# A graph kernel's edge counts with packed block words, a wait for the pair ahead, and degree sums by DMA

## The reference

```python
edge_index = jnp.stack([src, dst])
# layer 0: an MLP on each edge, batch norm over all edges, sum by target
edge_features = jnp.concatenate([x[src], x[dst]], axis=1)
h = edge_features @ W1.T + b1
h = jax.nn.relu(_batchnorm(h, g1, be1))      # mean and variance over the edges
h = h @ W2.T + b2
edge_updates = jax.nn.relu(_batchnorm(h, g2, be2))
x_out = jax.ops.segment_sum(edge_updates, dst, num_segments=x.shape[0])
# layers 1 to 3: GCN forward and backward, four resonant steps, 8-head attention over the same edges
x = _layernorm(x + layer(x, edge_index), axis=-1)
```

## Time and profile before

| | us |
| --- | --- |
| median of three runs | 4106.11 |
| profiled execution, its own time | 4105.13 |
| its span | 4103.4 |
| counts, from 80 to | 849 |
| aggregation, to | 977 |
| edge stage, to | 1469 |

### The profile page before, as it was taken

One profiled execution on the slowest core, in us unless ns is written; L12 is line 12 of the kernel. 1 busy time (PEld: TensorE's weight loads), 2 busy tenths in 40 slices (PEclk: granted clock), 3 DMA queues, 4 the chain that ended last, 5 costly groups with the idle time before them and its releaser, 6 DMA issues. The chain is left out here.

```text
span 4103.4 us, 83720 instructions
## 1 busy us (share of the span) xinstructions
PE 3401.6 (83%) x20358; PEld 1667.9 (41%) x20359; DVE 2769.9 (68%) x3759; ACT 1589.8 (39%) x2188; POOL 1042.3 (25%) x1132
## 2 busy tenths in 40 slices
PE   3777777677899978888989994898899989979995
PEld 1333333333444557777455553333322233332223
DVE  6887766622666666664121215899799989989995
ACT  2134555520222246553011111311288831218883
POOL 2887774565666412220000001000100000000000
PEclk8989999978999999998999996999899999989998
DMA  2245665667777668776747774211144331113343
GB/s 62 89 160 189 215 226 191 215 210 248 248 251 242 222 228 252 233 212 193 263 136 253 251 258 98 88 56 56 50 136 141 115 95 56 56 38 117 108 132 70
DMA packets 359412, 662.49 MB, mean 161 GB/s; under 512 B 134549, under 2 KB 221715, under 8 KB 358545
## 3 DMA queue, kind: packets, MB, share of 16 engines
q1 hardware_dynamic: 236288, 360.99, 27.9%
q10 hardware_dynamic: 97940, 248.84, 17.6%
q0 software_dynamic: 25088, 51.43, 4.8%
HBM read 428.22 MB, written 208.17 MB: 155 GB/s over the span
## 5 line engine op out<-in xcount | busy, mean ns | idle before, releaser
L836 POOL DMA_INDIRECT gat<-a_table,gidx x592 | 674.9, 1140 | 246.8 <-issue 143.8
L1754 DVE SCALAR_TENSOR_TENSOR pw<-ex,c_full 128x1564 f32<-128x1564 f32 x400 | 680.8, 1778 | 35.7 <-ACT ex L1278 31.0
L1278 ACT ACTIVATE ex<-psum 128x782 f32<-128x782 f32 x800 | 610.3, 826 | 77.3 <-PE psum L2194 58.5
L1716 DVE CUSTOM_DVE_ANT_0 masked<-psum,masks 128x1784 bf16<-128x1784 f32 x320 | 552.4, 1784 | 64.0 <-ACT masks L1251 43.4
L1803 PE MATMUL psum<-one_src,one_dst 128*128 x1968 | 418.8, 353 | 208.0 <-DVE one_dst L1437 116.8
L1435 DVE TENSOR_SCALAR one_src<-iota_sub,src_low 128x800 f16 x984 | 382.0, 429 | 194.1 <-PE psum L1803 111.4
L2203 PE MATMUL psum<-pw,vaug 128*32 128x391 f32 x3200 | 348.7, 508 | 29.8 <-DVE pw L1754 9.5
L1803 PEld LDWEIGHTS psum<-one_src,one_dst 128*128 x1968 | 189.7, 100 | 421.3 <-issue 338.0
L1251 ACT ACTIVATE masks<-masks,far 128x3128 bf16<-128x3128 bf16 x40 | 115.4, 2900 | 424.6 <-DMA masks<-ct_parts 424.6
L1083 ACT ACTIVATE r<-psum,vec 128x1024 f32<-128x1024 f32 x98 | 118.1, 1205 | 369.0 <-PE psum L1954 361.0
L1437 DVE SCALAR_TENSOR_TENSOR one_dst<-row_c,window_at,iota_row 128x256 f16 x492 | 233.4, 474 | 0.0
(11 more groups left out here) (355 smaller groups left out, 4859.5 us busy)
## 6 DMA issues: line engine op xcount, KB each, us to landing
c_full<-c_whole SPq DMA_DIRECT2D x80, 977.5 KB, 5.1
r_edges<-r ACTq DMA_DIRECT2D x98, 512.0 KB, 4.8
r_in<-r_edges ACTq DMA_DIRECT2D x98, 512.0 KB, 3.9
c_ring<-ct_parts SPq DMA_DIRECT2D x100, 480.0 KB, 4.4
c_whole<-c_sum ACTq DMA_DIRECT2D x100, 400.0 KB
a_edges<-gat SPq DMA_DIRECT2D x148, 256.0 KB
a_in<-a_edges ACTq DMA_DIRECT2D x74, 512.0 KB, 4.4
c_ring<-ct_parts SPq DMA_DIRECT2D x100, 320.0 KB, 3.6
```

Source lines behind the costliest of these rows:

```text
L836: g.indirect_dma_start(to, None, a_table, bass.IndirectOffsetOnAxis(ap=gidx[:, s, k:k + 1], axis=0)).then_inc(landed, 16)
L1278: a.activation(ex[:, step_slot(n // 2), (n % 2) * 2 * CW:(n % 2 + 1) * 2 * CW].rearrange("p (h t) -> p h t", h=2), psum[:, o:o + 2 * BANK] ...
L1716: v.tensor_tensor_reduce(out=masked[:, n % 2, 0:count * width].rearrange("p (c t) -> p c t", c=count), in0=psum[:, first * BANK:(first + c ...
L1754: v.scalar_tensor_tensor(pw[:, step_slot(k), :].rearrange("p (h t) -> p h t", h=HQ), ex[:, step_slot(k), :].rearrange("p (h t) -> p h t", ...
```

## The change

- `block_tab` loses the row with the pairs before a window. DVE loads four packed words with one load for four windows, and takes the number of pairs so far from a register (`total_dve`). PE loads one word with the lengths of three windows (`length_tab`), and counts in `total_pe`.
- `one_hots` has a new first line: `hold("dve", dve, S["one_ready"], before + p)`. DVE's sequencer begins a pair only when VectorE has completed the one ahead.
- `ROUNDS` is 20: 120 groups are staged first, and 28 late ones follow among and behind the direct ones. The late and direct groups read their indices straight from `src_i`, with no copy by POOL.
- The two halves of the first product are made in the prologue (PE, and two copies on ACT).
- The degrees go through DRAM: ACT stores both rows, waits, and loads each back to 128 partitions; the matmuls that spread them go, and PE's aggregation follows the first small matmul of the stage. DVE makes the roots first and sums when the rows are back, beside the aggregation. Behind the last matmul stand three DVE operations.

```diff
-ROUNDS = 22
+ROUNDS = 20
...
+        def pairs_before(eng, total):
+
+            return nc.s_assert_within(eng.snap(total), PAIR0, PAIR0 + NWIN * NPAIR)
...
             act.wait_ge(S["ab_high"], NB)
+            for k, half in enumerate((y, z)):
+                act.wait_ge(S["halves_psum"], k + 1)
+                a.activation(half[:, :], psum[:, 0:NP], ACT.Copy).then_inc(S["halves_taken"], 1)
             act.wait_ge(S["weff_ready"], 1)
...
             load_rows(0)
+            act.dma_start(degree_rows[0:1, :].rearrange("o (a c) -> (o a) c", c=SUB), degs[:, :]
+                          ).then_inc(S["degrees_stored"], 16)
+            act.wait_ge(S["degrees_ready"], 1)
+            act.dma_start(degree_rows[1:2, :].rearrange("o (a c) -> (o a) c", c=WN), target_degrees
+                          ).then_inc(S["degrees_stored"], 16)
+            act.wait_ge(S["degrees_stored"], 32)
+            for j, to in enumerate((out_degrees, in_degrees)):
+                act.dma_start(to[:, :], degree_rows[j:j + 1, :].broadcast_to([P, NP])).then_inc(S["degrees_back"], 16)
...
             def one_hots(w, p, before):
                 slot = (before + p) & (PAIRS - 1)
+                hold("dve", dve, S["one_ready"], before + p)
                 dve.wait_ge(S["slot_free"], before + p + 1)
...
             def count_four(i):
-                done_pairs = None
+                words = nc.values_load_multi_w_load_instructions(
+                    block_tab[0:1, 2, ds(4 * i, 4)], engines=[dve.engine], min_val=0, max_val=NPAIR * 512 + NPAIR)[1]
                 for q in range(4):
+                    first = nc.s_assert_within(dve.snap(words[q] & 511), 0, NPAIR - 2)
+                    end = nc.s_assert_within(dve.snap(words[q] >> 9), 2, NPAIR)
+                    before = nc.s_assert_within(dve.snap((pairs_before(dve, total_dve) - first) & 65535), PAIR0 - NPAIR,
+                                                PAIR0 + NWIN * NPAIR)
                     w = 4 * i + q
-                    first, end, before = window(dve, w, done_pairs)
-                    done_pairs = before + end
                     one_hots(w, first, before)
                     with dve.Fori(first + 1, end) as p:
                         one_hots(w, p, before)
+                    dve.reg_add(total_dve, total_dve, end - first)
...
             def count_group(g, ms):
...
+                    if m % SETS == 0:
+                        word = pe.value_load(length_tab[0:1, ds((GROUP // SETS) * g + m // SETS, 1)], min_val=0,
+                                             max_val=NPAIR << 9 * (SETS - 1) | NPAIR << 9 | NPAIR)
+                    length = nc.s_assert_within(pe.snap((word >> 9 * (m % SETS)) & 511), 2, NPAIR)
...
-            for k in range(2):
-                after(pe, S["halves_taken"], k)
-                feature_rows(W["W1"][:, k * P:(k + 1) * P], z, S["halves_psum"])
```

More of the change, by code:

```diff
@@ L96 @@
 AHEAD = 4
-ROUNDS = 22
-LATE = [(8 * j + s) for j in (22, 23) for s in range(SLOTS)] + [8 * 24 + s for s in range(4)]
+ROUNDS = 20
+LATE = [(8 * j + s) for j in range(ROUNDS, NU // 4) for s in range(SLOTS)] + [8 * (NU // 4) + s for s in range(4)]
 assert NG == 196 and LATE[-1] == NG - 1
@@ L282, in gnn @@
         hp = sb("hp", [P, 2, NP], f16)
+        at[0] = after_ring
+        in_degrees = sb("in_degrees", [P, NP], f32)
+        below_top()
         at[0] = after_ring
@@ L833, in take_rows, with fetch_rows, gather @@
                 g.tensor_copy(gidx[:, s, :], src_i[:, ds(4 * group, 4)]).then_inc(S["row_sb"], 1)
[L835 to L839, removed]
+            def fetch_rows(to, rows, landed):
+                g.indirect_dma_start(to, None, a_table, bass.IndirectOffsetOnAxis(ap=rows, axis=0)).then_inc(landed, 16)
+            def gather(i, counted=None, least=0, spread=(0,) * SLOTS, last=False):
                 first = isinstance(i, int) and i == 0
@@ L845, in gather @@
                         take_rows(8 * i + (s + 1), s + 1)
-                    else:
-                        take_rows(next_group if next_group else 8 * i + 8, 0)
+                    elif not last:
+                        take_rows(8 * i + 8, 0)
                     if not first:
@@ L864, in _ @@
                 gather(i)
-            gather(ROUNDS - 1, next_group=SLOTS)
+            gather(ROUNDS - 1, last=True)
             order = []
@@ L870, in _ @@
                     order += [(None, m) for m in range(AHEAD)]
-                elif AHEAD <= j < len(LATE):
+                elif j >= AHEAD:
                     order.append((None, j))
+            order += [(None, m) for m in range(NU // 4, len(LATE))]
             def group_of(n):
@@ L1786, in _ @@
                          start=True, stop=True).then_inc(S["ab_ready"], 1)
+            pe.wait_ge(S["ab_taken"], NB)
+            for k in range(2):
+                after(pe, S["halves_taken"], k)
+                for c, w in CHUNKS:
+                    last = t.matmul(psum[:, c:c + w], W["W1"][:, k * P:(k + 1) * P], z[:, c:c + w], start=True, stop=True)
+                last.then_inc(S["halves_psum"], 1)
+            pe.wait_ge(S["halves_taken"], 2)
             pe.wait_ge(S["consts_ready"], 1)
@@ L1831, in count_group @@
                     known = isinstance(w, int)
-                    first, end, before = window(pe, w, done_pairs)
-                    done_pairs = before + end
+                    if m % SETS == 0:
+                        word = pe.value_load(length_tab[0:1, ds((GROUP // SETS) * g + m // SETS, 1)], min_val=0,
+                                             max_val=NPAIR << 9 * (SETS - 1) | NPAIR << 9 | NPAIR)
+                    length = nc.s_assert_within(pe.snap((word >> 9 * (m % SETS)) & 511), 2, NPAIR)
+                    before = pairs_before(pe, total_pe)
                     after(pe, S["lo_made"], w + -2)
-                    count_pair(m % SETS, first, before, True)
+                    count_pair(m % SETS, 0, before, True)
                     if not (known and w < 2):
@@ L1839, in count_group @@
                         source_degrees(w + -3, (m - 3) % 4)
-                    with pe.Fori(first + 1, end) as p:
+                    with pe.Fori(1, length) as p:
                         count_pair(m % SETS, p, before, False)
+                    pe.reg_add(total_pe, total_pe, length)
                     t.matmul(bank(2 * (m % SETS), 1), zerosb[:, 0:P], zerosb[:, 0:1], start=False, stop=True,
```

114 lines of the change are left out of this document (46 added, 68 removed).

## The result

The changed kernel takes 4226.6 us (median of 4 runs, 4223.6 to 4230.2) against 4110.6 (4104.8 to 4115.8): ratio 1.0283, 95% interval 1.0262 to 1.0303. It is slower by 116 us where the forecast was 4159 us, an increase of 53, and it lies outside the range of 4100 to 4205. The profiled execution took 4223.6 us with a span of 4221.9.

What follows compares the result with a forecast made beforehand. PE set the pace of the counts before; DVE was to become the bound. 4105.1 + 1.5 (prologue) + 111 (counts) - 39 (aggregation) - 20.5 (edge stage) = 4158, with the median 1 us above: 4159 us, range 4100 to 4205.

Steps and rivals of the forecast that it cites:

- The bound moves to DVE: Counts: DVE needs 863 us against PE's 700, so DVE replaces PE as the bound.
- The gap, 0.35 us: Counts, DVE: idle time behind each pair's end from the new wait, 0.35 us, making a pair cost 1.53 us.
- the counts' term: Count stage: it grows by 111 us, between +40 and +190.
- Changes of window, 110 us: Counts, DVE: 75 changes of 0.6 us and 25 of 2.6 us, together 110 us, bounds 60 and 150.
- The pair, 1.18 us: Counts, DVE: a pair alone, without the gap behind it, takes 1.18 us.
- PE needs 700 us: Counts, PE: it saves about 0.7 of its 1.9 us a window and needs 700 us.
- Prologue: Prologue: ACT's two copies behind PE's matmuls exceed its slack before DVE's call, +1.5 us (0 to 4).
- aggregation: Aggregation: PE starts sooner, pauses 9.5 us behind five tiles, and fewer operations follow: -39 us, bounds -48 and -28.
- edge stage: Edge stage: PE's waits for POOL's direct groups go, with some slow matmuls behind them: -20.5 us (-15 to -23).
- PE starts at its lower clock: Aggregation: with the gather holding up tiles, the case for the smaller gain, -28 us.
- The first: Rival, counts: the wait costs nothing that counts and PE stays the bound, 3982 us, chance 0.14.
- The third, PE's clock: Rival, counts: PE waits for each pair and its clock falls toward 1.2 GHz, +25 us, 4184, chance 0.10.

Runs made afterwards that it cites:

- e1: The changed kernel without the new wait, so a pair may begin while the one ahead is still under way: 4036.0 us.
- e4: The kernel before the change with the new wait alone (old words, 22 rounds, old aggregation): 4294.3 us.
- e2: The changed kernel with the new wait moved behind the wait for `slot_free`: 20 us faster than the changed kernel.
- e7: The kernel before the change with the packed words and running totals alone: 45 us faster than the kernel before in its group.
- e11: The changed kernel with the wait aimed one pair back, in the first twelve windows alone, and POOL's holds in the counts one round lower: 3985.7 us, ratio 0.9700.
- e3: The changed kernel with the new wait aimed at the pair before the last one, as many waits as before: 4035.7 us.
- e5: The changed kernel with the wait for the pair before the last one in the first four windows alone (82 pairs): 4001.8 us.
- e6: e5 with POOL's own holds in the counts one round lower (28 pairs, 9 windows): 3999.5 us.
- e8: e5 with 22 staged rounds instead of 20: 45 us above e5.

## Why the prediction was wrong

*The bound moves to DVE.* Right, and of its size shown by e1 and e4.

*The gap, 0.35 us.* This step failed. It measured 0.46, and 491 x 0.11 = 54 us of the 61 that the counts' term is short. I took the edge stage's 0.665 and said that the pair's instructions are those of that row less the two of the loop's start. They are not: behind the new wait stands one register row more, that of line 1450, which waits for `slot_free`. The deduction itself was right. From start to start the edge stage's gap is 0.04 us to the release, then 0.10 to the loop's move, 0.07 to its FUSED_REGOPS, 0.24 to the second wait, 0.08 to the address and 0.14 to the TENSOR_SCALAR; without the two middle ones, 0.31, it is 0.355. That is what e2 measured, which has as many rows as are left here, and the extra row makes it 0.46. It could be seen ahead of the run: the order of the changed kernel's instructions lists a REGISTER_ALU of line 1450 and one of line 1452 behind the wait for `one_ready`. The bound that I gave the range, 0.45, was also too low, though the text's own upper end was 0.665: with it the range would have held the time.

*Changes of window, 110 us.* Near, 6 us short. The 342.3 us of idle time less 491 x 0.46 = 226 leave 116. In e4, with the old words, 364.8 less 226 leave 139: the words save 23 us for DVE.

*The pair, 1.18 us.* Right: DVE's pairs run from 85.5 to 1009.1, 923.6 us, less 342.3 is 581, and by 492 is 1.18.

*PE needs 700 us.* Near: 687 in e7, with all that POOL and ACT make it wait for.

*Prologue, aggregation, edge stage.* +3.0 for +1.5; -35.3 for -39, as the first 70 matmuls of the aggregation took 16.25 us where I had put 14, at a granted clock of 0.69 in 1024 to 1060 us (the bound "PE starts at its lower clock"); and -21.5 for -20.5, of which 16 are in the edge stage and 5.5 behind it, where the kernels differ by some us without a reason that I can name. That the -21.5 comes so close to the -20.5 is thus in part luck. POOL's first direct fetch begins 19 us ahead of the stage, as forecast. That POOL ends in time was right in this kernel, with nothing to spare: its last fetch begins 21 us ahead of the stage's end, and PE's 1.6 us of waiting for ACT's `r` are the first sign of POOL being late.

*The rivals.* The first (the wait costs nothing, 3982 us) is refuted as a mechanism by e1. e11 comes near its number, 3985.7, with another wait (one pair back, in twelve windows) and POOL's holds lowered, which says nothing for it. The Trainium skill, "VectorE: DVE Perf Modes", section "The DRAIN you can't avoid", by which a semaphore behind each operation costs nothing, led there; with a wait behind which a second wait's count and an address are worked out the trace shows 0.46 us a pair, and with the wait aimed one pair back (e3) 5.6 us in all. The third, PE's clock, did not occur: the granted clock was 0.94 in the whole run, as before, and 0.90 in the counts where it had been 0.92; a matmul of a pair took 359 ns in the mean where it had taken 353. That the stages' terms would each depend on where POOL stands was in none of the rivals.

## What to carry to other kernels

A wait on an engine's own last result costs the row-by-row work that its sequencer has to do behind it. List these rows one by one from the order of the instructions, and when you take a gap from another stage as the measure, compare the two lists row by row. Multiply by the number of waits before you compare with the bound of today; an engine that is idle for a quarter of a stage can't give that time if the idle time lies elsewhere. If such a wait is there to let another engine breathe, aim it one step back, and use it only where the engine runs unbroken. And when a helper engine becomes faster, look for its own holds: they can swallow the gain until they are moved as well.

## What the runs showed of the hardware

A POOL fetch can be held up for tens of us while DVE's operations overlap without a break. In the kernel before the fetch ran from 88.09 to 137.02. DVE around that end:

```profile
135.06 0.75 DVE L1435 TENSOR_SCALAR one_src<-iota_sub,src_low 128x800 f16 x2
135.73 0.47 DVE L1437 SCALAR_TENSOR_TENSOR one_dst<-row_c,window_at,iota_row 128x256 f16 x1
136.30 0.92 DVE L1435 TENSOR_SCALAR one_src<-iota_sub,src_low 128x800 f16 x2
```

Each TENSOR_SCALAR had begun 0.40 us behind the start of the operation ahead, 0.08 before its end. At 136.30 it began 0.57 behind for the first time, 0.10 past the end at 136.20, and the fetch ended 0.82 us behind that end. In e5 the waits stopped behind four windows, and there a fetch ended likewise at 217.91, 0.82 us behind the end at 217.08 of the last operation of the chain (POOL, then DVE):

```profile
191.41 26.50 POOL L841 DMA_INDIRECT gat<-a_table,gidx  x1 [0.30 <-DVE one_dst L1455]
```
```profile
216.60 0.48 DVE L1455 SCALAR_TENSOR_TENSOR one_dst<-row_c,window_at,iota_row 128x256 f16 x1
217.21 0.88 DVE L1453 TENSOR_SCALAR one_src<-iota_sub,src_low 128x800 f16 x2
```

The same 0.82 us stand in e1, e6 and e8; in e7 its fetch of 56.4 us ended 0.82 us behind an operation whose successor was not late, so a break is not always needed. In e3, at nearly the same pace, now and then a TENSOR_SCALAR begins 0.43 or 0.44 us behind in place of 0.40, still before the end of the operation ahead, and no fetch in its first windows took over 2 us:

```profile
102.36 0.48 DVE L1454 SCALAR_TENSOR_TENSOR one_dst<-row_c,window_at,iota_row 128x256 f16 x1
102.79 0.76 DVE L1452 TENSOR_SCALAR one_src<-iota_sub,src_low 128x800 f16 x2
103.47 0.48 DVE L1454 SCALAR_TENSOR_TENSOR one_dst<-row_c,window_at,iota_row 128x256 f16 x1
103.91 0.82 DVE L1452 TENSOR_SCALAR one_src<-iota_sub,src_low 128x800 f16 x2
```

The Trainium skill, "SBUF — State Buffer", section "Who interferes with whom", says that a VectorE operation that uses the pair of ports shared with GpSimd (one in a two-port mode, or one with two inputs in SBUF against a GpSimd instruction that reads SBUF) holds them for its whole length if it came first, and that GpSimd is blocked meanwhile. No run here shows which ports these operations use. The rows fit the rule, and add that POOL's wait outlasted not one operation but a chain of them: 24 pairs in e5, 45 before and 54 in e1. That the small late starts, and nothing else about the waits, spare POOL this is only read from these rows; no run set them apart.

POOL's last 304 fetches, the same instructions in each kernel with 20 rounds, took between 470 and 485 us from the first direct one. What differs is POOL's waiting for fetches to land: 106 us in the changed kernel with its 470, 121 in e2 with 485. Why they land later there is open. In e11, where these fetches began earlier, they took 500 us, of which POOL stood 21 us in waits for PE to come within four steps.
